# Last pass of a MetaFormer block on one core: loads moved from SyncE's to ScalarE's queue, with a fourth buffer

## What is computed

```python
x = x + _L0_conv_ref(_ln_c(x), w1, b1, gamma, beta, w2, b2)      # involution, 49 taps
t = _to_tokens(x)                                                # 16 * 3136 tokens of 64
t = t + _L0_ffn_ref(_ln_t(t), Wg, bg, W1, b1, W2, b2)            # top 2 of 8 experts
x = _from_tokens(t, x)                                           # back to b, c, h, w
```

## Time and profile before

| | |
|---|---|
| median of the runs | 2416.89 us (2396.77 to 2417.44) |
| the profiled execution | 2408.16 us, span from first to last instruction 2406.4 us |
| TensorE busy | 1961.1 us (81% of the span) |
| VectorE busy | 1501.7 us (62%) |
| ScalarE busy | 841.2 us (35%) |
| GpSimd busy | 937.3 us (39%) |
| mean rate of the DMA engines | 197 GB/s |
| last stage | from 2308.6 us to the end, 97.8 us (4% of the span) |

### The profile page before, as it was taken

The page is one execution under the profiler, slowest core; times in us unless marked ns, Lnnn a source line. Parts: engine busy times, 40 slices in busy tenths (PEclk is TensorE's granted clock), DMA queues, the critical chain, the costliest instruction groups (busy, mean ns, idle before and its releaser), DMA issues. The chain is left out here.

```text
span 2406.4 us, 34530 instructions
## 1 busy us (share of the span) xinstructions
PE 1961.1 (81%) x10208; PEld 1212.0 (50%) x10208; DVE 1501.7 (62%) x2687; ACT 841.2 (35%) x1540; POOL 937.3 (39%) x977
## 2 busy tenths in 40 slices
PE   4992888997989999998999985308898889988934
PEld 3761444444545455555555545306666666666623
DVE  2441665665878878787788876625666556666623
ACT  2540111111222213222122223206666666666700
POOL 6000000000234332343323437755777777777720
PEclk9995998999999999999999995559999999999955
DMA  7768777777777777777777733138888888888658
GB/s 224 159 134 179 178 192 184 177 189 187 208 193 203 213 199 190 199 211 202 194 193 199 197 95 110 54 99 245 255 251 246 244 245 249 250 251 242 212 161 267
DMA packets 291481, 474.18 MB, mean 197 GB/s; under 512 B 120156, under 2 KB 196059, under 8 KB 268327
## 3 DMA queue, kind: packets, MB, share of 16 engines
q1 hardware_dynamic: 258055, 439.69, 68.0%
q0 software_dynamic: 28832, 30.65, 4.6%
q10 hardware_dynamic: 4416, 1.73, 0.3%
HBM read 392.67 MB, written 81.93 MB: 197 GB/s over the span
## 5 line engine op out<-in xcount | busy, mean ns | idle before, releaser
L954 POOL DMA_INDIRECT token_rows<-gate_rows,gate_index x392 | 412.7, 1053 | 980.4 <-DVE gate_index L1273 866.7
L1153 DVE TENSOR_TENSOR prod<-z_ps,r_all 119x896 f32<-119x896 f32 x512 | 545.2, 1085 | 184.4 <-PE z_ps L1066 159.0
L1485 POOL DMA_INDIRECT mixed<-exp_mix,exp_xt x474 | 483.9, 1021 | 215.0 <-issue 134.6
L1070 PE MATMUL z_ps<-xq,band 112*119 112x448 f32 x1024 | 440.9, 568 | 37.5 <-DVE prod L1153 37.4
L1508 ACT ACTIVATE exp_hid<-exp_h_ps,exp_pack 128x384 f32<-128x384 f32 x632 | 331.8, 579 | 21.7 <-PE exp_h_ps L1552 20.1
L1552 PE MATMUL exp_h_ps<-exp_tok,exp_pack 128*128 128x384 f32 x1264 | 272.3, 359 | 65.5 <-issue 60.0
L1070 PEld LDWEIGHTS z_ps<-xq,band 112*119 112x119 f32 x1024 | 186.1, 190 | 245.2 <-issue 182.6
L1552 PEld LDWEIGHTS exp_h_ps<-exp_tok,exp_pack 128*128 128x128 f32 x1264 | 221.1, 194 | 162.1 <-issue 156.4
L986 ACT ACTIVATE ob<-o_ps 128x448 f32<-128x448 f32 x64 | 34.9, 545 | 623.0 <-PE o_ps L1083 623.0
L1564 PE MATMUL exp_y_ps<-exp_hid,exp_pack 128*64 128x384 f32 x1264 | 242.8, 506 | 0.0
L1083 PE MATMUL o_ps<-prod,pick 119*32 119x448 f32 x2048 | 241.2, 564 | 0.9 <-DVE prod L1153 0.3
(11 more groups left out here) (194 smaller groups left out, 2130.7 us busy)
## 6 DMA issues: line engine op xcount, KB each, us to landing
xq<-xs SPq DMA_DIRECT2D x192, 896.0 KB
exp_pack<-packs SPq DMA_DIRECT2D x316, 321.5 KB
exp_xt<-token_rows SPq DMA_DIRECT2D x158, 120.0 KB
xs<-xpad SPq DMA_DIRECT2D x32, 448.0 KB, 5.7
xin<-in_x_dram SPq DMA_DIRECT2D x8, 1568.0 KB, 11.4
co<-ob SPq DMA_DIRECT2D x512, 24.5 KB
merge_yt<-mixed SPq DMA_DIRECT2D x28, 448.0 KB, 5.0
mixed<-exp_mix,exp_xt POOLq DMA_INDIRECT x474
```

The costliest lines, as they stand in the source:

```text
L954: pool.indirect_dma_start(out=token_rows[:, :], out_offset=bass.IndirectOffsetOnAxis(ap=index[b % RR][:, j:j + 1], axis=0), in_=rows[b % R ...
L1070: mm = nc.tensor.matmul(zt, band[t % BR][rows_in, at:at + MF], maps, start=True, stop=True)
L1153: nc.vector.tensor_tensor(prod[(NU * t + u) % PR][:, :, :].rearrange("p m (d x) -> p m d x", d=D), z_ps[(NU * t + u) % 3][0:MF, :, 0:CN].r ...
L1485: pool.indirect_dma_start(out=mixed[:, :], out_offset=bass.IndirectOffsetOnAxis(ap=xt[t % XT][:, j, ROW_ID:ROW_ID + 1].bitcast(U32), axis= ...
```

## The change

The loads leave SyncE's program and become a program of ScalarE, in the same order and with the same kind of wait. SyncE keeps the stores alone. `RING` becomes 4, which gives both `yt` and `res` a fourth buffer (and each a fourth semaphore); a load then waits for the transposes four steps back, and VectorE for the stores four steps back.

```diff
     DUAL = CHUNKS // 2
-    RING = 3
+    RING = 4
@@
-            def load(d):
-                if d >= RING:
-                    sp.wait_ge(turned, d - RING + 1)
-                sp.dma_start(yt[d % RING][:, :, :].rearrange("p j x -> p (j x)"),
-                             mixed[2 * CHUNK * d:2 * CHUNK * (d + 1), :]
-                             .rearrange("(p j) c -> p (j c)", p=P)).then_inc(yt_in[d % RING], 16)
@@
-            for d in range(DUAL + 2):
-                if d < DUAL:
-                    load(d)
-                if d >= 2:
-                    store(d - 2)
+            for d in range(DUAL):
+                store(d)
             for i in range(RING):
                 sp.wait_ge(res_out[i], sum(runs[i::RING]) * 16)
+
+        @block.scalar
+        def _(act):
+            def load(d):
+                if d >= RING:
+                    act.wait_ge(turned, d - RING + 1)
+                act.dma_start(yt[d % RING][:, :, :].rearrange("p j x -> p (j x)"),
+                             mixed[2 * CHUNK * d:2 * CHUNK * (d + 1), :]
+                             .rearrange("(p j) c -> p (j c)", p=P)).then_inc(yt_in[d % RING], 16)
+
+            for d in range(DUAL):
+                load(d)
```

## The result

| | before | after |
|---|---|---|
| median of 11 runs | 2403.56 us (2396.77 to 2417.44) | 2383.97 us (2375.42 to 2393.81) |
| span of the profiled execution | 2406.4 us | 2378.0 us |
| last stage | 97.8 us | 74.1 us |
| of it head / body / tail | 5.08 / 87.15 / 5.57 us | 4.9 / 61.6 / 7.6 us |

The changed kernel takes 0.9911 of the time before (95% interval 0.9889 to 0.9932), 21 us less, with 16 to 27 in the interval. Of these, 13.3 are the base and say nothing of the change: with 11 runs the median of before is 2403.56 us, that much lower than the one the forecast started from.

A forecast was written before the change was run, and what follows sets the result against it. Loads, kept back behind stores in SyncE's program, set the last stage's pace. Head 5.08, body 77.7 and tail 5.57 make 88.4 us against 97.8, so 2416.89 - 9.4 = 2407.5 us, range 2387 to 2418.

The forecast's parts named there:

- what bounds the kernel, and what a load waits for: Last stage: loads set the pace; load 10, held behind store 7's pieces in SyncE's program, would go out 3.98 us earlier.
- the engines' order: Last stage: TensorE 2.22, VectorE 1.09, SyncE 1.71 us a step, all below 2.52; issuing loads from ScalarE costs 0.
- rival 4: Last stage: loads don't start earlier because ScalarE is held up; time as before, 2416.9 us; chance 0.02.
- TensorE's 2.22 us: Last stage: time between TensorE's starts of steps 8 and 9, taken as its pace with its data there.
- what the DMA engines then give: Body of the last stage: 319 GB/s makes 2.88 us a step, 77.7 us in all, 9.4 less.
- the tail: Last stage, from last addition to end: stays at 5.57 us, with at most 1.4 us more for a store left over.
- rival 1: Last stage: transfers are the bound anyway, only the hole at the start closes; 3.3 us less, 2413.6 us; chance 0.22.
- Three or four loads under way: Last stage: this many loads under way at nearly all times, so the holes close and the DMA engines are the bound.
- The fourth `res` buffer. Cost 0: Last stage: the buffer gains nothing now, as VectorE waits only for TensorE; it gives stores a step more of delay.
- Rival 3: Body of the last stage: the rate goes to the best stretch's 364 GB/s; gain 19.1 us, 2397.8 us; chance 0.10.
- Rival 2: Body of the last stage: two queues lower the rate; 2421.6 us in mild form, 2436.6 us in severe; chance 0.11.
- The rule weighed there: Last stage: issuing from two engines saves only the sequencer's time; by it alone the gain is about 3.3 us.

The follow-up runs named there:

- four and eight: The changed kernel with four buffers for the loads (`yt`) and eight for the results (`res`): stage 69.6 us, 0.9890 of the time before.
- full stores: Stores sent from all 128 partitions, 32 DMAs in place of 80: stage 67.3 us in the changed kernel, 83.5 us in the kernel before.
- Half loads: Kernel before with all on SyncE's queue, ten buffers, load d behind store d - 9, each load issued as two DMAs of 64 partitions: stage 92.7 us.
- paired loads: Kernel before, one queue on SyncE, each load bringing two steps (896 KB): stage 78.7 us with six to seven steps ahead, 77.6 us with up to eleven.
- two and two: The changed kernel with two buffers for loads and two for results, on two queues: stage 98.5 us.

## Why the prediction was right and wrong, step by step

**Right: what bounds the kernel, and what a load waits for.** The loads set the pace and stood behind stores. The body of the changed kernel is at a share of 1.01, TensorE's waits for loads are gone but for three, and load 3 goes out right behind the first three, 1.34 us after the first, as forecast. The buffer alone gave nothing, as the order says it must.

**Right: the engines' order.** ScalarE's start cost nothing (head 4.9 us for 5.08), so rival 4 is out, and no engine's arithmetic became the bound: a step takes 61.6 / 27 = 2.28 us. But the prediction misread TensorE's 2.22 us as its own pace with its data there. The rows of steps 8 and 9 say that both waited for a load, and load 9 landed at 2338.85 us, just ahead of step 9. TensorE's own work in such a step is the 1.76 us of the row, at a granted clock of 0.50. Steps of 2.04 us (four and eight buffers, clock 0.80) and 2.15 us (full stores, clock 0.60) bear that out. The clock isn't what made the stage shorter either: the kernel with full stores had 0.60 in its body and the shortest stage, the changed one 0.68, the one before 0.52.

One engine came closer than the forecast had it. SyncE was to need 1.71 us a step for its stores. In the changed kernel it issues them in one stream:

```profile
2309.91 65.19 SPq L1682 DMA_DIRECT2D out_dram<-merge_res  x80
```

Of this it spends 60.7 us inside the issues, 2.17 us a step, and waits 2.9 us for additions after the first. One in 0.65 us, as with stores alone, would be 52 us; so the issues got longer where the queues were full, and the DMA engines' limit and SyncE's aren't cleanly apart here. With 32 stores of 128 partitions, where SyncE waits 51.8 us, the body goes from 376 to 409 GB/s.

**Wrong: "what the DMA engines then give".** This is the term that failed. I took 319 GB/s, with 364 as the bound from above, and 27 x 2.88 = 77.7 us. The body had 378 GB/s and 61.6 us, 16.1 us less than forecast. That is more than the 14.3 us by which the forecast of the stage was off; the tail took 2.0 back. I read the best stretches of the trace as the limit of the DMA engines. They were only the best that a queue with 1.2 MB under way gave for 3 us. The change that closes the holes also puts more bytes in line, 2.2 MB in place of 1.2, and the rate rises with that, up to 411 GB/s. The share didn't tell it: 0.89 left room for a ninth, and the gain in rate was a third. That a share is no rate I had written in rival 1 (it also counts packets that wait), as an argument for a smaller gain, and not the reverse: that a share of 1 could be worth far more. The runs show it worth anything from 229 to 411 GB/s. "Three or four loads under way" was too high as well: with one load in 2.28 us and 6.1 us to land there are 2.7.

The trace of before held a warning that I cut away with stretches of 3 us. By 1 us, it reads:

```profile
2323.00:2324.00 1.00, 0.14 (x1) 0.00 (x0) 0.82 (x1) 0.00 (x0) 0.00 (x0) 0.50 1.04 402
2324.00:2325.00 1.00, 0.84 (x4) 0.84 (x5) 0.27 (x1) 0.00 (x0) 0.00 (x0) 0.50 1.04 412
```

The highest 3 us of the changed kernel have 416 GB/s, close to it. Such a short stretch can serve as a bound and no more: the one from 2321 to 2322 us has a share of 1.19 and 260 GB/s. As a bound from above 412 GB/s gives 27 x 2.23 = 60.2 us of body, and 26.9 us of gain. By the way I set the low end, the lowest run less the gain, the range would have gone down to 2396.77 - 26.9 = 2369.9 us and held the result.

**Wrong: "The fourth `res` buffer. Cost 0".** It gave 4.1 us, beside the fourth load buffer's 2.1, in single profiles. I had read that VectorE never waited for stores in the kernel before and priced the buffer by that row. But I had also written that stores may need the step of delay. With loads out of the way stores are what VectorE waits for, 28.4 us, and the buffer count sets how many bytes are in line. A sign of it had been named among those of the changed profile: VectorE waiting for stores.

**Wrong in size: the tail.** I took 0 and at most 1.4 us more; it grew by 2.0. I had priced the stores left over at 319 GB/s. Stores alone run at 242 there, about what their issues allow, a piece in 0.65 us or 247 GB/s.

**The rivals.** Rival 3 (2397.8 us, chance 0.10) was the nearest, a gain of 19.1 us where 23.7 were found in the stage. Rival 1 is out: the rate didn't stay. Rival 2 is out: loads and stores mixed run at 407 and 411 GB/s, so loads beside stores aren't slow as such. The stretch of 2365 to 2368 us that spoke for it, at 185 GB/s, isn't explained by a thin queue either: it had 1.1 MB under way, hardly less than the one at 364 GB/s (1.2 MB).

**The rule weighed there.** The Trainium skill, DMA: Bandwidth & Descriptors, section "Issuing engines are not separate DMA queues", has it that a second issuing engine saves the sequencer's time alone, usually small beside the transfer. The runs can't tell the sequencer's time from the order of its program: the second queue gave 16.7 us with three and three buffers, and it takes both away at once. They don't agree that the time is small: 108 issues on one queue are 70 us of a stage of 78, and 28 more made it 92.7.

**The rule I should have weighed.** Half loads alone ran at 229 GB/s and full loads at 406, both with full DMA engines. SBUF — State Buffer, section "Door 1: The DMA port swizzle", of the Trainium skill says that partitions 0 to 63 reach only 8 of the 16 ports on the side of the DMA engines, with some 218 GB/s as their limit and 436 for all 128. The trace agrees in part: loads of 64 partitions had 229 GB/s, 5% over that limit, with the two halves in turn in the queue; but stores of 64 partitions alone, also halves in turn, had 247 on one queue and 273 on two, a quarter over it. By this rule the stores alone at the end of the stage would be slow for their form. The runs don't show that for one queue, since there the issues already hold them at 247. What they show for the form is 273 GB/s with two queues of 64 partitions against 397 with one of 128.

**Open.** How much of the line from 1.2 to 2.9 MB is latency that is covered, and how much is that half stores need something of the other half beside them, isn't separated. The two kernels with full stores lie near the same line, which speaks for the first; stores of 128 partitions alone, at 397 GB/s with 1.6 MB, and the paired loads, at 341 with 2.3, lie well off it, one above and one below. What held the paired loads back stays open too. A layout of `base` in which the two halves are two images, so that a store of 128 partitions is also the right output, wasn't tried.

## What to carry to other kernels

Before a transfer is taken out of another's way, ask what the change does to the number of bytes under way, and take the upper bound of the rate from the shortest stretches with a full share, not from the average of the long ones. A second queue is worth its issue time and the freedom of order; here it gave 16.7 us with three buffers on each side, 23.7 with four, 28.2 with four and eight, and with two and two it was level with one queue that had three. Where transfers cover 64 partitions and nothing full runs beside them, 229 to 273 GB/s were left here of some 400.

## What the runs showed of the hardware

- One queue moved loads and stores mixed at 407 GB/s for 15 us, and loads alone at 406, so a single queue can fill the 16 DMA engines. With paired loads it had only 341 GB/s over 63 us, at 2.3 MB under way.
- A share of the DMA engines near 1 went with 229, 334, 378 and 411 GB/s. It doesn't tell the rate.
- Back-to-back stores of 64 partitions cost SyncE 0.65 us each, stores of 128 partitions 0.332 us (median, changed kernel with full stores), and loads issued by ScalarE 0.326 us each in the changed kernel. With stores of 64 partitions alone on two queues a piece took over 1 us to issue on either. Where the queues were full single ones became longer, up to 1.73 us on SyncE in the changed kernel and 1.58 us on ScalarE with loads alone.
- Loads of 64 partitions alone ran at 229 GB/s where loads of 128 partitions gave 406, both with full DMA engines.
